# Local attention layers as one software pipeline over tiles, with the division of the attention weights on GpSimd

## The reference, cut to what matters

```
h = shift_token(x);  q, k, v = split(h @ wqkv)          # 8 heads of 64
q = l2norm(q) * qs;  k = l2norm(k) * ksc;  q, k = rotary_xpos(q, k)
# windows of 64 queries that see their own and the previous 64 keys, masked
sim  = 8 * q @ k^T   ;  attn = softmax(sim)  ;  o = attn @ v
x = x + o @ wo
h = layernorm(shift_token(x)) @ w1 + b1 ; a, g = split(h)
x = x + (a * gelu(g)) @ w2 + b2
```

## Time and profile before

| | |
|---|---|
| runs of the kernel before | 3057.51 us median of 3 (3056.97 to 3065.76) |
| the profiled execution's own time | 3055.92 us |
| its span, first to last instruction | 3054.1 us |
| mean granted TensorE clock | 0.847 |
| busy: PE, PEld, DVE | 2275.5 us (75%), 1277.1 us (42%), 1975.2 us (65%) |
| busy: ACT, POOL | 1416.0 us (46%), 560.6 us (18%) |
| the two passes of the first local layer | from 565.74 us (first rotary product) to 667.79 us (last `xf`) |
| the two passes of the second | from 705.88 us to 804.44 us |

### The profile page before, as it was taken

The page is one execution under the profiler, slowest core; times in us unless marked ns, Lnnn a source line. Parts: engine busy times, 40 slices in busy tenths (PEclk is TensorE's granted clock), DMA queues, the critical chain, the costliest instruction groups (busy, mean ns, idle before and its releaser), DMA issues.

```text
span 3054.1 us, 46022 instructions
## 1 busy us (share of the span) xinstructions
PE 2275.5 (75%) x17392; PEld 1277.1 (42%) x17392; DVE 1975.2 (65%) x4104; ACT 1416.0 (46%) x2537; POOL 560.6 (18%) x336
## 2 busy tenths in 40 slices
PE   4798588577779668767759948867767985885766
PEld 4576122254547412245546712225353751222545
DVE  5855696655674489565656568946566556966565
ACT  1333277264533347554623416746263332782544
POOL 0242000213043200041205300012212420003130
PEclk9999599778879879978779968978777985997878
DMA  3000200101000100010000020010100002001010
GB/s 132 1 1 1 74 16 9 28 6 26 11 9 1 53 22 19 8 27 11 21 17 1 1 69 19 7 22 16 22 17 8 1 1 74 16 9 30 5 26 18
DMA packets 52016, 65.13 MB, mean 21 GB/s; under 512 B 17696, under 2 KB 29216, under 8 KB 51264
## 3 DMA queue, kind: packets, MB, share of 16 engines
q1 hardware_dynamic: 48584, 56.18, 7.3%
q10 hardware_dynamic: 3192, 5.80, 0.6%
HBM read 25.19 MB, written 15.01 MB: 13 GB/s over the span
## 4 chain that ended last, share of the span: by engine, by line
PE 49%; DVE 23%; ACT 12%; DMA 6%; issue 5%; SPq 3%; POOL 2%; ACTq 0%; DVEq 0%; POOLq 0%
PE PS L1136 44%; DVE arena L971 9%; ACT arena L616 5%; DMA tmp<-xf 3%; ACT arena L571 2%; PE PS L1415 2%; PE PS L1154 1%; DVE s_at L1027 1%; DMA scr_k<-arena 1%; DVE tmp L996 1%; POOL arena L437 1%; DMA arena<-scr_k 1%; PE PS L1480 1%; SPq L344 1%; DVE arena L1044 1%
## 5 line engine op out<-in xcount | busy, mean ns | idle before, releaser
L1136 PE MATMUL PS<-arena 128*32 128x256 f32 (+4 forms) x10240 | 825.3, 356 | 204.4 <-DMA arena<-scr_k 75.3
L971 DVE TENSOR_REDUCE arena<-PS 128x1 f32<-128x512 f32 x1024 | 642.0, 684 | 101.7 <-PE PS L1136 101.7
L571 ACT ACTIVATE arena<-PS 128x1024 f32<-128x1024 f32 x512 | 515.6, 1033 | 306.7 <-PE PS L1136 306.7
L1136 PEld LDWEIGHTS PS<-arena 128*32 128x32 f32 (+4 forms) x10240 | 313.0, 124 | 714.9 <-DVE arena L971 282.9
L1136 PE MATMUL PS<-wqkv,arena 128*128 128x512 f32 x384 | 221.1, 730 | 65.4 <-ACT arena L602 56.2
L1136 PEld LDWEIGHTS PS<-w2e,arena 128*128 128x128 f32 x2048 | 246.0, 192 | 52.0 <-issue 51.7
L527 ACT ACTIVATE arena<-PS 128x512 f32<-128x512 f32 x256 | 150.7, 597 | 245.1 <-PE PS L1136 245.0
L1136 PE MATMUL PS<-w2e,arena 128*128 128x128 f32 x2048 | 246.8, 275 | 0.1
L616 ACT ACTIVATE arena<-PS,arena 128x128 f32<-128x128 f32 x512 | 230.0, 527 | 16.0 <-DVE arena L1079 16.0
L917 DVE TENSOR_TENSOR arena<-PS,arena 128x512 f32<-128x512 f32 x128 | 86.1, 689 | 213.2 <-PE PS L1136 212.8
L601 ACT ACTIVATE arena<-PS 128x1024 f32<-128x1024 f32 x64 | 65.5, 1023 | 325.1 <-DVE s_at L1027 248.5
(11 more groups left out here) (274 smaller groups left out, 3463.7 us busy)
## 6 DMA issues: line engine op xcount, KB each, us to landing
arena<-arena SPq DMA_DIRECT2D x120, 128.0 KB, 2.3
arena<-scr_k SPq DMA_DIRECT2D x28, 200.0 KB
arena<-scr_q SPq DMA_DIRECT2D x28, 192.0 KB
scr_q<-arena SPq DMA_DIRECT2D x16, 256.0 KB, 3.0
scr_k<-arena SPq DMA_DIRECT2D x16, 256.0 KB, 5.2
x_in<-in_x SPq DMA_DIRECT2D x5, 512.0 KB, 4.0
scr_q<-arena ACTq DMA_DIRECT2D x8, 256.0 KB, 4.9
scr_k<-arena ACTq DMA_DIRECT2D x8, 256.0 KB, 5.8
```

What stands on the lines that cost most here:

```text
L571: act.activation(pb[:, n % 8], pair(2 * (n % 2)), ACT.Exp).then_inc(S["p"], 1)
L971: dve.tensor_reduce(mxp[:, h % 2, j, t, hf:hf + 1], PS[:, ring_bank("mx", h, n), :], AX, ALU.max)\
L1136: return pe.matmul(o, w, v, start=start, stop=stop, **kw)
```

## The change

The two passes become one loop. Step `j` runs from -3 to 11, and in a step each engine does its part for different tiles. PE: `qkv(j+3)`, `outputs(j-3)` (weights times v), `scores(j+1)`, `kq(j+2)`, `project(j-3)`, `turn(j-1)` (transposes of the weights). DVE: `xf(j-4)` and what belongs to it, `norms(j+2)`, `divide(j-1)`, `rotate(j+3)`, `maximum(j+1)`. ACT: the exponentials of tile j, the copies of j-3, j-2, j+3 and j+2, the square of j+3. POOL: the power of j+2, the division of j-1, the scaling of k of j+2, the rotary sum of j+3.

Besides the order, four things change:

- The weights are multiplied by 1/sum on POOL (128 x 1024 elements, new line L433) instead of on DVE (old L1071).
- The reciprocal square root is one power of -0.5 on POOL (128 x 16 elements a tile, new line L428) in place of ACT's square root with its table and DVE's reciprocal; the Newton step stays on DVE and is now done for each tile.
- ACT copies both halves of the transposed weights (new L621) instead of one.
- PSUM: q and k of the tile have one pair of banks instead of two, v one instead of two, the scores one pair instead of two; the transposes of q and k share two banks with those of the weights. `qk_a` has 2 buffers instead of 4 and the squares 1 instead of 2.

```diff
@@ POOL
                 for l in range(DEPTH):
-                    for t in range(T + 2):
-                        u = l * T + t
-                        if t < T:
-                            v = qk_a[u % 4]
+                    for j in range(-3, T + 1):
+                        t, u = j + 2, l * T + j + 2
+                        if 0 <= t < T:
+                            pool.wait_ge(S["ssq_ok"], u + 1)
+                            pool.tensor_tensor(rq[:, t], ssq[:, t], sc[:, 11:12].broadcast_to([P, 2 * HL]), ALU.pow).then_inc(S["rq0"], 1)
+                        if 0 <= j - 1 < T:
+                            m = l * T + j - 1
+                            pool.wait_ge(S["rl"], m + 1)
+                            v = pl[:, m % 2]
+                            pool.tensor_tensor(v, v, bc(rl[:, m % 3], [P, 2, 4, KEYS], 3), ALU.mult).then_inc(S["pn"], 1)
+                        if 0 <= t < T:
+                            pool.wait_ge(S["rot"], u + 1)
+                            pool.wait_ge(S["rqe"], u + 1)
+                            v = qk_a[u % 2][:, INNER:].rearrange("p (h c) -> p h c", c=DL)
+                            pool.tensor_tensor(v, v, bc(rq[:, t, HL:], [P, HL, DL], 2), ALU.mult).then_inc(S["qkr"], 1)
+                        t, u = j + 3, l * T + j + 3
+                        if 0 <= t < T:
+                            v = qk_a[u % 2]
                             pool.wait_ge(S["rotb"], u + 1)
                             pool.tensor_tensor(v, v, qk_b[u % 2], ALU.add).then_inc(S["rot"], 1)
...
@@ ACT
+                    for j in range(-3, T + 3):
+                        if 0 <= j < T:
+                            exps(j)
+                        t, u = j - 3, l * T + j - 3
+                        if 0 <= t < T:
+                            act.wait_ge(S["o_lps"], u + 1)
...
+                            act.copy(olT[:, u % 2], PS[:, 7, :].rearrange("p (c n) -> p c n", c=4)).then_inc(S["olT"], 1)
+                        t, u = j - 2, l * T + j - 2
+                        if 0 <= t < T:
...
+                            for r in range(2):
+                                act.wait_ge(S["pt_ps"], 2 * u + r + 1)
+                                act.copy(pt[:, u % 2, r], PS[:, 5 + r, :].rearrange("p (c n) -> p c n", c=4))\
+                                    .then_inc(S["ptd" if r else "pt"], 1)
...
                             act.wait_ge(S["rotb"], u + 1)
-                            if u >= 2:
-                                act.wait_ge(S["ssq"], u - 1)
-                            act.activation(qk_sq[u % 2], pair(2 * (t % 2)), ACT.Square).then_inc(S["sq"], 1)
...
+                            if u >= 1:
+                                act.wait_ge(S["ssq"], u)
+                            act.activation(qk_sq, pair(2), ACT.Square).then_inc(S["sq"], 1)
@@ DVE
+                    def norms(t):
+
                         u = l * T + t
...
+                        y, v, w = rq[:, t], ssq[:, t], rqt[:, t]
+                        dve.wait_ge(S["sq"], u + 1)
+                        dve.tensor_reduce(v, qk_sq.rearrange("p (h c) -> p h c", c=DL), AX, ALU.add).then_inc(S["ssq"], 1)
+                        dve.wait_ge(S["ssq"], u + 1)
+                        dve.tensor_scalar(v, v, 1e-24, None, ALU.max).then_inc(S["ssq_ok"], 1)
+                        dve.wait_ge(S["rq0"], u + 1)
+                        link(dve.scalar_tensor_tensor(w, y, -0.5, y, ALU.mult, ALU.mult))
+                        link(dve.tensor_tensor(w, w, v, ALU.mult))
+                        dve.scalar_tensor_tensor(y, w, 1.5, y, ALU.add, ALU.mult).then_inc(S["rqe"], 1)
+
+                    def divide(t):
+
+                        m = l * T + t
+                        dve.wait_ge(S["p_exp"], 8 * (m + 1))
+                        dve.reciprocal(rl[:, m % 3], sl[:, m % 3]).then_inc(S["rl"], 1)
...
-                            link(dve.reciprocal(rl[:, m % 3], sl[:, m % 3]))
-                            v = pl[:, m % 3]
-                            dve.tensor_tensor(v, v, bc(rl[:, m % 3], [P, 2, 4, KEYS], 3), ALU.mult).then_inc(S["pn"], 1)
...
+                        if 0 <= j + 2 < T:
+                            norms(j + 2)
+                        if 0 <= j - 1 < T:
+                            divide(j - 1)
+                        if 0 <= j + 3 < T:
+                            rotate(j + 3)
+                        if 0 <= j + 1 < T:
+                            maximum(j + 1)
@@ PE
+                        for i, bank in enumerate((2, 3, 4)):
+                            if t and i == 0:
+                                pe.wait_ge(S["rotb"], u)
+                                pe.wait_ge(S["sq"], u)
+                            if t and i == 2:
+                                pe.wait_ge(S["vl"], u)
...
+                    for j in range(-3, T + 3):
+                        if 0 <= j + 3 < T:
+                            qkv(j + 3)
...
+                        if 0 <= j - 3 < T:
+                            outputs(j - 3)
+                        if 0 <= j + 1 < T:
+                            scores(j + 1)
...
+                        if 0 <= j + 2 < T:
+                            kq(j + 2)
+                        if 0 <= j - 3 < T:
+                            project(j - 3)
+                        if 0 <= j - 1 < T:
+                            turn(j - 1)
```

More of the change, by code:

```diff
@@ L196, in build @@
         kT = take([4, WIN + N])
-        qT = take([4, N])
+        qT = take([2, 4, P])
         vl = take([T, INNER])
@@ L205, in build @@
         rl = take([3, 2, 4])
-        after = used[0]
-        pl = take([3, 2, 4, KEYS])
+        pl = take([2, 2, 4, KEYS])
         pt = take([2, 2, 4, P])
+        hT = take([N])
+        qk_a = [take([2 * INNER]) for _ in range(2)]
+        qk_sq = take([2 * INNER])
         olT = x_in[:].rearrange("p (q c) n -> p q c n", c=4)
[L210 to L215, removed]
+        qk_b = [v[:].rearrange("p t w -> p (t w)") for v in (s_at, tmp2)]
         used[0] = 4 * (WIN + N)
@@ new lines, in exps @@
+                    def exps(t):
+                        n = l * T + t
+                        act.wait_ge(S["ml"], n + 1)
+                        if n >= 2:
+                            act.wait_ge(S["pt_ps"], 2 * (n - 1))
+                        for r in range(2):
+                            for c in range(4):
+                                h = 2 * c + r
+                                act.activation(pl[:, n % 2, r, c], PS[:, r, KEYS * c:KEYS * c + KEYS],
+                                               ACT.Exp, bias=ml[:, n % 2, r, c:c + 1], scale=rq[:, t, h:h + 1],
+                                               accum_out=sl[:, n % 3, r, c:c + 1]).then_inc(S["p_exp"], 1)
@@ L662, in link @@
                 dve.wait_ge(S0["dve0"], k0[0])
+            link(dve.memset(sc[:, 11:12], -0.5))
             link(dve.tensor_copy(identb[:], ident[:]))
@@ new lines, in outputs @@
+                    def outputs(t):
+                        m = l * T + t
+                        pe.wait_ge(S["pt"], m + 1)
+                        pe.wait_ge(S["ptd"], m + 1)
+                        pe.wait_ge(S["vz%d" % t], 16 * (2 if t else 1) * (l + 1))
+                        if t:
+                            pe.wait_ge(S["xf"], 2 * T * l + t)
+                        for c in range(4):
+                            for b2 in range(2):
+                                for r in range(2):
+                                    h = 2 * c + r
+                                    ins = mm(PS[64 * r:64 * r + 64, 7, P * c + 64 * b2:P * c + 64 * b2 + 64],
+                                             (vl if b2 else vz)[:, t, DL * h:DL * h + DL],
+                                             pt[:, m % 2, r, c, 64 * b2:64 * b2 + 64], tile_position=(0, 64 * r))
+                        ins.then_inc(S["o_lps"], 1)
@@ new lines, in turn @@
+                    def turn(t):
+                        m = l * T + t
+                        pe.wait_ge(S["pn"], m + 1)
+                        for r in range(2):
+                            if t + 3 < T:
+                                pe.wait_ge(S["kq"], 2 * (m + 3) + r + 1)
+                            else:
+                                pe.wait_ge(S["ptd" if r else "pt"], m)
+                            for c in range(4):
+                                ins = pe.transpose(PS[:, 5 + r, P * c:P * c + P], pl[:, m % 2, r, c], ident[:])
+                            ins.then_inc(S["pt_ps"], 1)
```

252 lines of the change are left out of this document (79 added, 173 removed).

## The result

| | before | after |
|---|---|---|
| time, median us (lowest to highest) | 3057.24 (3053.24 to 3065.76) | 3110.39 (3103.10 to 3118.48) |
| profiled execution, its span | 3055.9, 3054.1 | 3118.5, 3116.2 |
| first rotary product to last `xf` of a local layer, first / second layer (mean of 4) | 101.0 / 98.6 | 112.2 / 112.0 |
| last `xf` of the first layer to first rotary product of the second | 38.0 | 31.5 |

The change makes the kernel slower: ratio 1.0171, 95% interval 1.0137 to 1.0204. The forecast was 2992 us, and faster. Each of the 8 layers takes some 12.3 us more; the way from the first layer to the second takes 6.5 us less.

What follows compares the result with a forecast made beforehand. No engine bounds a local layer; the order in which they wait for each other decides. 4 x (4.2 + 3.0 + 2 x 4.4) = 64 us won from 3055.9 gives 2992 us, range 2940 to 3075.

Steps and rivals of the forecast that it cites:

- p: Duration of POOL's power instruction (L428) for a tile: taken as 1.0 us, ends 0.31 and 2.35, paid 60 times.
- rival 2: POOL's power at L428 is dear, with DVE's queue behind it; slower from 2.07 us on, 3112 at 3.0; chance 0.20.
- The sign that it named for being wrong: The forecast counts as wrong if L428 isn't near 1 us, or L1045's starts are spaced by something other than POOL's chain.
- The ring: Loop step through DVE's norms, POOL's division, scaling and rotary sum, then the bias: 8.6 + p = 9.6 us.
- The second ring: Loop step through scaled k, second half of `kq`, copy, square and next `norms`: 8.2 + p, longest only without the lock.
- The hold of the bias: DVE's small bias instruction (L1068) waits until POOL's rotary sum (L443) ends, lasting up to 2 us instead of 0.17.
- Rival 3: The bias slips in before POOL's rotary sum, 4.4 us a layer, 35 in all: 2957 us; chance 0.08.
- The clock: PE's granted clock is near 1.00 from the first division to the last `project`; PE idles some 1.7 us a step.
- the tail: Chain through PE, ACT and DVE from the copy of tile 7's scaled keys to the last `xf`: 22.5 us.
- step 5: First layer's loop step without a new tile: 0.5 + 7.0 us to tile 7's scaled keys, copied by 641.1.
- Rival 4: PE's clock stays low while the loop fills, 2.7 us in each of 8 layers: 3014 us; chance 0.08.
- The end of the layer: Shift DMAs no longer queue up: tile 6 lands 1.2 us after the last `xf`, not 5.6; 4.4 us won each layer.

Runs made afterwards that it cites:

- first experiment: The kernel after, with POOL's power replaced by a multiplication by 1e-9 of the same shape and place: 2969.71 us, ratio to before 0.9712.
- the second: The kernel after, with the inverse root on DVE (bit-shift seed, three Newton steps) and no power on POOL: 3039.80 us, ratio to before 0.9949.
- the seventh experiment: The kernel after, with POOL's rotary sum replaced by three clearings of the same 1024 elements: 3105.03 us, ratio to before 1.0150.
- experiments 9: The kernel after, with the inverse root on DVE in two Newton steps and POOL scaling k ahead of its division: 2984.72 us, ratio to before 0.9753.
- experiment 12: The kernel with root on DVE in two Newton steps and k's scaling first, plus POOL's rotary sum waiting for the bias: 2971.30 us, ratio 0.9731.
- experiment 11: The kernel after, with POOL scaling k ahead of its division and its rotary sum replaced by three clearings: 3059.53 us.

## Why the prediction was wrong, point by point

**The price of the power is the term that failed.** The sum's term p was put at 1.0 us and measured 2.905. The prediction took p = 1.0 from "the shortest arithmetic POOL does", and as its upper end 2.35, "unless a power costs over sixty times an addition for each element". It does: 0.158 us against 0.0026 us ((2.35 - 1.04) / 512), sixty times, and 0.38 us besides. (Those two rows are not of one form: 2.35 is a sum of two full inputs, 1.04 a product with an input that is repeated. Between two products of the same form, 1.90 and 1.04 us, it is 0.0017 us an element, and the power's is over ninety times that.) The first experiment shows that p decides the sign (2970 us with p = 0.217), the second that it is the power and not the root's place in the ring (3040 us with DVE's longer row). The right chance was that of rival 2, at 0.20: place, queue behind it and the point from which it decides, 2.07, are as it said. Its formula gives 2992 + 1.905 x 60 = 3106 us for p = 2.905; the profiled execution took 3118.5 and the median was 3110.4; that it comes so near is in part luck (see the clock, below). The sign that it named for being wrong, L428 not near 1 us, is the one that came. What was wrong was the bound: a row of a clearing and a row of a sum can't bound an operation that neither of them does.

**The ring was right, its terms were not all.** Predicted 8.6 + 2.9 = 11.5 us, measured 10.4 to 10.65. The division takes 1.90 us, not the 2.35 of the rotary sum (0.45 less), and from POOL's power to its division it is 3.72 us, not 3.96. The second ring, 8.2 + p less that same 0.45 = 10.65, was right to within what the steps differ by; the prediction named it but let it count only without the hold.

**The hold of the bias was right, and its worth was not.** L1068 takes 1.573 us in the median (0.166 to 1.879). Of its 64 rows 55 are held, 48 of them to the end of the rotary sum (L443) and 7, in the tails, to the end of the division or of k's scaling; beside the 9 short ones POOL does nothing. Rival 3 put 35 us on its absence, 4.4 us a layer; the seventh experiment measured 5, with clearings that take 0.55 us longer than the sum and hold the bound instead, so it is no clean price of the hold alone. With the power gone from POOL and the other ring shortened, the same hold was worth some 13 us by the medians (experiments 9 and 12).

By the Trainium skill (SBUF — State Buffer, "Who interferes with whom") a DVE instruction with two SBUF inputs contends with a GpSimd instruction that reads SBUF and not with one that only writes, and tensor_scalar in its two-port mode contends with either. The traces agree in each case: the bias is held by the sum (1.87 us) and not by the clearings (0.17), and the bound, a tensor_scalar, is held by the sum (0.83, experiment 12) and by the clearings (up to 0.89, experiment 11).

**The clock.** I took PE's full clock from the first division on. The stage 603.6 to 647 has 0.92, the tail of this layer 1.00, but in other layers the tail has less. The tails of the first and of the seventh layer of the launch, from the last sum of squares to the last `xf` (columns as in the earlier trace rows):

```profile
641.60:676.10 34.50, 21.13 (x358) 18.49 (x356) 9.97 (x31) 20.11 (x66) 16.16 (x8) 1.00 0.04 8
2892.00:2933.90 41.90, 30.21 (x357) 26.36 (x355) 10.26 (x31) 20.11 (x66) 16.16 (x8) 0.73 0.03 6
```

At a clock of 1.00 the tail takes 34.5 us, at 0.73 it takes 41.9; ACT and POOL are busy for the same 20.11 and 16.16 us in both, and PE for 21.1 against 30.2. By the prediction's sum the last sum of squares starts 0.5 us into step 5, at 633.0, and the tail takes 663.6 - 633.0 + 1.9 = 32.5; the mean of the 8 is 38.0. That is 8 x 5.5 = 44 us too little, and 2.0 of the 5.5 are missing at the full clock too. The seven steps of the first layers were summed 633.0 - 569.3 + 6 x 1.9 = 75.1 us long; in the second the last sum of squares comes at 715.0 + 2 x 8.3 + 3 x 9.6 + 9.9 + 0.5 = 770.8, and the steps take 770.8 - 708.3 + 7 x 1.9 = 75.8. Measured are 70.6 in the mean: 4 x (4.5 + 5.2) = 39 us too much. The formula came as near as 12 us to the profiled execution only because these two nearly cancel. Rival 4 looked for the clock in the fill of the loop; there the clock was low indeed, 0.69, but the steps are shorter than predicted (9.78 against 10.2). With a cheap power the same omission shows: the formula gives 2945 us for p = 0.217 and measured were 2970, although the steps are shorter than its 8.8; the tails are 35.7 us long in the mean where the sum has 32.5 - 2.7 = 29.8.

**The end of the layer was right.** Predicted 4.4 us a layer; the gaps behind a layer (last `xf` to the next layer's first rotary product) shrank by 6.5 us (38.0 to 31.5) behind the first and by 2.8 us behind the second (498.8 to 496.0, means), 4.7 in the mean.

## What to carry to other kernels

An operation that no row shows has no upper bound from rows of other operations: give its dear case the weight that ignorance deserves, and before moving it into a ring ask what the other engine would need (here eight or five small DVE instructions at 0.21 us against a wait of 3.0). In a ring of waits look for the second ring of nearly the same length, since opening one alone gave 5 or 18 us here and opening both gave 51. Where a short instruction of one engine is held until a long one of another ends, order them so that the long one waits for the short one.

## What the runs showed of the hardware

- A power on POOL (two inputs, 32 bit) takes 2.905 us for 16 elements a partition and 1.642 us for 8; a multiplication of the same shape takes 0.217 us.
- POOL's product of 1024 elements with an input repeated along its last axis takes 1.90 us, the sum of two full inputs 2.35 us.
- A clearing of 1024 elements on POOL takes 0.95 to 0.98 us.
- A small DVE instruction with two inputs in the on-chip memory takes 0.17 us alone and up to 1.88 us beside POOL's sum, always to the sum's end; beside POOL's clearing it takes 0.17 us. A small tensor_scalar is held by either (0.83 us beside the sum, up to 0.89 beside a clearing).
